# The attention's softmax: eight exponentials from PSUM with the negated maximum as bias, and carries by DMA

## The chip, the cores and the metric

One core of a Trainium2 chip runs the whole kernel in one launch. The metric is the device time in microseconds. TensorE multiplies matrices, VectorE and ScalarE work on tensors and read and write both SBUF and PSUM, GpSimd works on SBUF, and SyncE here only issues DMAs.

## The reference

The input x has four sequences of 1024 tokens with 128 features. It is layer-normalised to xn, and the output is x + A(xn) + F(xn). A is a retention block of 16 heads (a causal decaying product without softmax, with group norms and a small MLP). F is two layers of windowed attention with an MLP; each layer computes:

```python
h = shift_token(x)                       # half of the features from the token before
q, k, v = split(h @ wqkv)                # 8 heads of 64
q, k = rotary_xpos(l2norm(q) * qs, l2norm(k) * ks)
sim = q @ k.T * 8, masked to a window of 64 and the 64 before it
o = softmax(sim) @ v
x = x + o @ wo
h = layernorm(shift_token(x)) @ w1 + b1
x = x + (a * gelu(g)) @ w2 + b2          # a, g are the halves of h
```

## The kernel before, in words

All five engines run hand-written queues that meet at semaphores. Time is tiled in 8 steps of 128 tokens, and a step has four slots, one for each sequence (k = 0 to 3). `run_bodies` goes over 8 steps of layer 0, 8 of layer 1, and two bodies that drain. A body works on three steps at once: `new` (projections), `old` (attention output) and `ff` (the MLP). In slot k each engine does, among other things, the projection of tile k of the new step, the scores of the tile two slots back (`turned`) and the weighting with values of the tile three slots back (`weighted`).

On TensorE a slot is, in order: transposes of the normalised q and k (`pe_turn`, line 1040), the value projection (1135), mask and scores into the PSUM tile pS (`pe_scores`, 1059 and 1072), transposes of the softmax weights into pT (1083), transposes of the attention output (1109), the q and k projection into pQK (1172), the output projection (`pe_wo`, 1115), and weights times values, into pS again (`pe_values`, 1098). Slot 0 has the MLP's matmuls besides (1234, 1245). `pe_values` of one tile needs pS after the softmax of the next tile has read it, and the next slot's `pe_scores` needs pS after `dve_output` has read it.

On VectorE a slot is: the maximum over each head's 128 scores and its subtraction (`dve_scores`, 757 and 759, PSUM to the SBUF tile pr), the residual (779), the sum of squares of q and k (724), the division by the softmax sum (`dve_output`, 767 and 769), and two rotations of pQK (711). The sum of squares waits for ScalarE's `Square` of pQK (550).

On ScalarE a slot is: copies of kT and qT from pT (510, 512), two carries, the shifted input of the next slot (489), two copies of the values (526, 527), the copy prT of the turned weights (534), the copy oT of the turned output (590), the `Square` (550), and one `Exp` of 1024 columns in place in pr (583). In slot 0 the exponential stands before the table load and the gelus (597). In layer 0, slot 3 has four `Identity` instructions (570) at its start and the retention block's squares and copies (607, 612) around the `Square`, and the exponential of slot 3 stands inside the retention block (634), which follows the slot on all engines. In that block TensorE starts with transposes of `aqk` (1269), which VectorE makes (858) from GpSimd's power (385) of those squares. In slot 1 of layer 1 ScalarE has two `Silu` with a bias (646) and a table load besides.

The carries keep the last 64 tokens of a tile's keys and values for the next step's window: 64 partitions of `vown` to `vmix` (517), and 64 columns of `kT` (518). The copy of the values (526) waits for the first, the copy of kT (510) for the second. GpSimd computes the reciprocal norms by a power and scales q and k (353 to 375). SyncE loads the inputs at the start, then in layer 1 one input tile and one output tile a step.

Of the kernel before, what the change touches and what calls it, by code (L numbers as in the profile page):

```python
# [12 lines left out]
P = 128  # L13
NB = 4
# [79 lines left out]
def program(nc, a, out):  # L94
    with ExitStack() as ctx:
# [129 lines left out]
        def score_bank(b):  # L225
# [12 lines left out]
        gn = [{n: sem(f"gn{k}_{n}") for n in ("agg", "dve", "mm", "var", "rs", "done")} for k in range(2)]  # L238
        LS = {n: sem(n) for n in (
            "carried", "v_kept", "h_ready", "qk_mm", "v_mm", "sq_done", "ss_done", "mul_done", "max_ss", "rn_done", "add_done",  # L240
            "qkn_done", "t_mm", "t_ev", "v_ev", "s_mm", "mx_done", "sub_done", "exp_done",
            "pt_mm", "pt_ev", "o_mm", "rec_done", "o_done", "ot_mm", "ot_ev", "wo_mm", "xr_carried", "xr_done", "hs",
            "ln_mm", "ln_bst", "ln_st", "ln_eps", "ln_rs", "hn_done", "hnt_mm", "hnt_ev", "ag_mm", "gelu_done",
            "hf_done", "w2_mm", "x2_done")}
# [53 lines left out]
            body(None, None, (1, NT - 1))  # L298


        @block.sync
        def _(sp):
            for b in range(NB):
                sp.dma_start(x[:, b, :, :], a["L0_attn_x"][b].rearrange("(t p) d -> p t d", p=P)).then_inc(x_ld[b], 16)
            sp.dma_start(tab[:, :, :, :], a["k_tab"]).then_inc(tab_ld, 16)
            sp.dma_start(wqkv[:, 0, :], a["L0_ffn_wqkv"][0]).then_inc(wqkv_ld, 16)
            for l in range(DEPTH):
                sp.dma_start(w1[:, l, :], a["L0_ffn_w1"][l]).then_inc(w1_ld, 16)
            sp.dma_start(wqkv[:, 1, :], a["L0_ffn_wqkv"][1]).then_inc(w_ld, 16)
            for l in range(DEPTH):  # L310
                sp.dma_start(wo[:, l, :, :], a["L0_ffn_wo"][l].rearrange("(c p) d -> p c d", p=P)).then_inc(w_ld, 16)
                sp.dma_start(w2[:, l, 0:2, :], a["L0_ffn_w2"][l, 0:2 * P, :].rearrange("(c p) d -> p c d", p=P)).then_inc(w_ld, 16)
                sp.dma_start(w2[0:CHUNKS[2][1], l, 2, :], a["L0_ffn_w2"][l, 2 * P:HID, :]).then_inc(w_ld, 16)

            sp.dma_start(xs[:, :, :], x_steps[0]).then_inc(G["xs"], 16)
            sp.wait_ge(G["osb"], 1)
            sp.dma_start(out_steps[0], osb[:, :, :]).then_inc(G["out"], 16)
            with sp.Fori(1, NT) as t:
                sp.wait_ge(G["out"], 16 * t)
                sp.dma_start(xs[:, :, :], x_steps[t]).then_inc(G["xs"], 16)  # L320
                sp.wait_ge(G["osb"], t + 1)
                sp.dma_start(out_steps[t], osb[:, :, :]).then_inc(G["out"], 16)
            sp.wait_ge(G["out"], 16 * NT)


        def pool_slot(eng, new, old, k):

# [164 lines left out]
        def act_slot(eng, new, old, ff, k):  # L492
# [12 lines left out]
            if turned:  # L505
                step, b, m = turned
                eng.wait_ge(S["t_mm"], 2 * m + 1)
                if not is_start(step):
                    eng.wait_ge(S["carried"], m - 3)
                eng.activation(kT[b][:, :, 0:P], pT[:, 512:1024].rearrange("p (c n) -> p c n", c=4), ACT.Copy).then_inc(S["t_ev"], 1)  # L510
                eng.wait_ge(S["t_mm"], 2 * m + 2)
                eng.activation(qT[:, :, :], pT[:, 0:512].rearrange("p (c n) -> p c n", c=4), ACT.Copy).then_inc(S["t_ev"], 1)
            if new:
                if not is_start(new):

                    need(eng, S["o_mm"], n - 3)
                    eng.activation(vmix[k][64:P, :, 0:DH], vown[k][64:P, :, 0:DH], ACT.Copy).then_inc(S["v_kept"], 1)
                    eng.activation(kT[k][:, :, P:P + WIN], kT[k][:, :, WIN:P], ACT.Copy).then_inc(S["carried"], 1)
                if k < NB - 1:
                    act_shift(eng, new, k + 1)  # L520

                eng.wait_ge(S["v_mm"], n + 1)
                if not is_start(new):
                    eng.wait_ge(S["v_kept"], n - 3)
                values = pV[:, :].rearrange("p (h d) -> p h d", h=H)
                eng.activation(vown[k][:, :, 0:DH], values, ACT.Copy).then_inc(S["v_ev"], 1)
                eng.activation(vmix[k][0:64, :, 0:DH], values[0:64], ACT.Copy).then_inc(S["v_ev"], 1)
# [9 lines left out]
            if ff and k == 0:  # L537
                eng.wait_ge(S["hnt_mm"], step_count(ff) + 1)
                eng.activation(hnT[:, :], pM[:, :], ACT.Copy).then_inc(S["hnt_ev"], 1)
            if k == NB - 1 and new and new[0] == 0:  # L540
                act_retention_project(eng, new[1], 0)
            if k == 0 and turned:
                act_exp(eng, b, m)
            if k == 0 and ff:
                act_load_table(eng, ACT.Gelu)
                act_gelu(eng, ff, 0)
# [11 lines left out]
            if k == NB - 1 and new and new[0] == 0:  # L558
                act_retention_project(eng, new[1], 1)
            else:  # L560
                if old and k == NB - 1:
                    act_shift_residual(eng, old)
                if k > 0 and turned:
                    act_exp(eng, b, m)

        def act_retention_in(eng, t):

# [11 lines left out]
            eng.activation(hs[64:P, :, :], xr[64:P, :, 0:P], ACT.Copy).then_inc(S["hs"], 1)  # L579

        def act_exp(eng, b, n):
            eng.wait_ge(LS["sub_done"], n + 1)
            eng.activation(pr[:, b % 2, :, :], pr[:, b % 2, :, :], ACT.Exp).then_inc(LS["exp_done"], 1)  # L583

        def act_output(eng, step, b):

# [39 lines left out]
        def act_retention(eng, t, old):  # L626
            for k in range(NB):
                n = 4 * t + k
                eng.wait_ge(A["t_mm"], n + 1)
                need(eng, A["qx"], n - 1)  # L630
                eng.activation(aqkT[:, k % 2, :, :], pM[:, 0:256].rearrange("p (g n) -> p g n", g=2),
                               ACT.Copy).then_inc(A["t_ev"], 1)
                if k == 0:
                    act_exp(eng, 1, count((0, t), 1))
                act_place_values(eng, t, k)
                if k + 2 < NB:
                    act_retention_project(eng, t, k + 2)
                if k == 0 and old:
                    act_shift_residual(eng, old)
            eng.wait_ge(A["y_mm"], 4 * t + 4)  # L640
            eng.activation(ayT, pY, ACT.Copy).then_inc(A["yt"], 1)
# [110 lines left out]
        def dve_scores(eng, b, n):  # L752
# [1 line left out]
            S = LS  # L754
            eng.wait_ge(S["s_mm"], n + 1)
            sc = pS[:, :].rearrange("p (h n) -> p h n", h=H)
            eng.tensor_reduce(mx[:, :], sc, AX.X, ALU.max).then_inc(S["mx_done"], 1)  # L757
            eng.wait_ge(S["mx_done"], n + 1)
            eng.tensor_tensor(pr[:, b % 2, :, :], sc, mx[:, :].unsqueeze(2).broadcast_to([P, H, P]),  # L759
                              ALU.subtract).then_inc(S["sub_done"], 1)  # L760

        def dve_output(eng, n):

# [279 lines left out]
        def pe_scores(eng, step, b, n):  # L1043
# [2 lines left out]
            evicted, subtracted, weighed = (counted(eng, v) for v in (2 * n + 2, n, n - 1))  # L1046
            eng.wait_ge(mask_done, 1)
            eng.wait_ge(S["t_ev"], evicted)
            need(eng, S["sub_done"], subtracted)
            need(eng, S["o_done"], weighed)  # L1050
            if b == 2:

# [33 lines left out]
        def pe_values(eng, b, n, turned):  # L1086
# [2 lines left out]
            eng.wait_ge(S["pt_ev"], n + 1)  # L1089
            eng.wait_ge(S["v_ev"], 2 * n + 2)  # L1090
            if turned:
                eng.wait_ge(S["sub_done"], n + 2)
            need(eng, S["o_done"], n)
            for i in range(H):
                g, j = i // 4, i % 4
# [125 lines left out]
        def pe_hidden(eng, step, chunks, turned, weighted):  # L1221
            S, l, ct = LS, step[0], step_count(step)
            for k in chunks:
# [3 lines left out]
                    if weighted:  # L1227
                        eng.wait_ge(S["pt_ev"], weighted[2] + 1)
                if k == 1 and turned:
                    eng.wait_ge(S["sub_done"], turned[2] + 1)  # L1230
                if k == 2:
                    eng.wait_ge(S["hf_done"], NC * ct + 1)
                for s in range(2):
# [190 lines left out]
```

## Time and profile before

| what | value |
|---|---|
| median of 3 runs | 990.7 us (988.4 to 990.86) |
| the profiled execution, its time | 988.95 us |
| its span, first to last instruction | 986.8 us |
| mean granted TensorE clock | 0.980 |
| TensorE busy | 868.8 us, 88% |
| VectorE busy | 685.1 us, 69% |
| ScalarE busy | 691.4 us, 70% |
| GpSimd busy | 623.8 us, 63% |

The profile is one execution. Its page has the busy time of each engine and groups of instructions by line; the trace behind it can be asked for who waited for whom, for windows, and for a timeline. A wait is put to the instruction that ended it. Durations of neighbouring instructions on one engine overlap, so the time that one really takes of its engine is from its start to the start of the next.

### The profile page before, as it was taken

How to read it: one execution, taken by the hardware profiler on the slowest of the kernel's cores; microseconds unless marked ns; L12 is line 12 of the kernel's file. 1: busy time of each engine (PE TensorE's matmuls, PEld its weight loads, DVE VectorE, ACT ScalarE, POOL GpSimd, SP SyncE). 2: the span in 40 equal slices, each digit the busy share in tenths (PEclk: the TensorE clock that was granted, in tenths of full speed). 3: DMA queues.
4: the chain of work that ended last, by engine and by line, in shares of the span. 5: the costliest groups of instructions: out<-in, count | busy, mean ns of one | idle time of the engine just before them, and what ended most of it. 6: DMA issues, size and time to landing. Idle time of an engine off the chain costs nothing.

```text
span 986.8 us, 26415 instructions
## 1 busy us (share of the span) xinstructions
PE 868.8 (88%) x10836; PEld 582.5 (59%) x10836; DVE 685.1 (69%) x1129; ACT 691.4 (70%) x1419; POOL 623.8 (63%) x492
## 2 busy tenths in 40 slices
PE   1678889989899998998989889999999999999876
PEld 0346666666656666566666656565656565656552
DVE  5874665757667576675666877888787878797733
ACT  0456786877868777687786667777777777777643
POOL 4488676776767767767576566657575757575500
PEclk9979999999999999999999899999999999999987
DMA  9100000000000000000000000000000000000000
GB/s 291 28 1 3 2 2 2 2 3 2 3 2 1 3 1 3 2 2 3 1 3 2 1 1 2 2 12 12 13 12 7 17 2 22 1 23 2 22 23 11
DMA packets 20481, 13.47 MB, mean 14 GB/s; under 512 B 4578, under 2 KB 19596, under 8 KB 20236
## 3 DMA queue, kind: packets, MB, share of 16 engines
q1 hardware_dynamic: 15108, 10.49, 3.5%
q10 hardware_dynamic: 5256, 1.31, 0.8%
q8 instruction: 87, 1.43, 0.6%
q14 instruction: 30, 0.25, 0.1%
HBM read 9.70 MB, written 2.10 MB: 12 GB/s over the span
## 4 chain that ended last, share of the span: by engine, by line
PE 51%; DVE 23%; ACT 14%; issue 8%; POOL 3%; DMA 1%; DVEq 0%; POOLq 0%; SPq 0%; ACTq 0%
PE pQK L1172 6%; DVE m L711 6%; PE pS L1098 5%; PE pT L1083 4%; PE pT L1040 4%; PE pM L1115 4%; PE pV L1135 4%; PE pM L1245 4%; PE pS L1072 4%; PE pQK L1336 3%; DVE xa L899 2%; DVE ss L724 2%; DVE pr L759 2%; DVE mx L757 2%; PE pS L1059 2%
## 5 line engine op out<-in xcount | busy, mean ns | idle before, releaser
L355 POOL TENSOR_TENSOR rn<-rn,half_neg 128x16 f32<-128x16 f32 x64 | 187.5, 2929 | 5.3
L368 POOL TENSOR_TENSOR m<-m 128x1024 f32<-128x1024 f32 x64 | 151.0, 2359 | 1.0 <-DVE m L711 1.0
L353 POOL TENSOR_SCALAR rn<-ss 128x16 f32<-128x16 f32 x64 | 16.3, 255 | 205.1 <-DVE ss L724 203.9
L375 POOL TENSOR_TENSOR qkn<-m,rn 128x1024 f32<-128x1024 f32 x64 | 123.7, 1933 | 5.0
L757 DVE TENSOR_REDUCE mx<-pS 128x8 f32<-128x1024 f32 x64 | 78.1, 1220 | 66.7 <-PE pS L1072 66.6
L1172 PE MATMUL pQK<-wqkv,hT 128*128 128x512 f32 x256 | 123.5, 606 | 0.8 <-DVE m L711 0.8
L510 ACT ACTIVATE kT<-pT 128x512 f32<-128x512 f32 x64 | 38.1, 595 | 86.4 <-PE pT L1040 85.9
L550 ACT ACTIVATE sq<-pQK 128x1024 f32<-128x1024 f32 x64 | 65.4, 1021 | 25.7 <-PE pQK L1172 25.6
L724 DVE TENSOR_REDUCE ss<-sq 128x16 f32<-128x1024 f32 x64 | 77.5, 1210 | 5.4 <-ACT sq L550 5.3
L1098 PE MATMUL pS<-vmix,prT 128*64 128x65 f32 x1024 | 74.0, 226 | 7.4 <-DVE pr L759 7.4
L1098 PEld LDWEIGHTS pS<-vmix,prT 128*64 128x64 f32 x1024 | 65.3, 139 | 25.5 <-issue 20.8
L759 DVE TENSOR_TENSOR pr<-pS,mx 128x1024 f32<-128x1024 f32 x64 | 78.4, 1225 | 2.2
L534 ACT ACTIVATE prT<-pT 128x1024 f32<-128x1024 f32 x64 | 65.1, 1017 | 18.4 <-PE pT L1083 17.9
L583 ACT ACTIVATE pr<-pr 128x1024 f32<-128x1024 f32 x64 | 67.7, 1058 | 13.6 <-DVE pr L759 12.6
L711 DVE TENSOR_TENSOR m<-pQK,rope 128x1024 f32<-128x1024 f32 x64 | 76.2, 1215 | 0.0
L1135 PE MATMUL pV<-wqkv,hT 128*128 128x512 f32 x128 | 69.8, 628 | 6.9 <-DVE gst L940 2.9
L711 DVE TENSOR_TENSOR m<-pQK,tab 128x1024 f32<-128x1024 f32 x64 | 75.4, 1210 | 0.0
L1098 PE MATMUL pS<-vown,prT 128*64 128x65 f32 x1024 | 74.2, 226 | 0.0
L1040 PE MATMUL pT<-cst,qkn 128*128 128x128 f32 x512 | 69.7, 280 | 4.6 <-POOL qkn L375 4.6
L1083 PE MATMUL pT<-cst,pr 128*128 128x128 f32 x512 | 69.9, 279 | 0.0
L1072 PE MATMUL pS<-kT,qT 64*64 64x128 f32 x2048 | 68.5, 272 | 0.0
L1234 PE MATMUL pT<-hnT,w 128*128 128x512 f32 (+1 forms) x128 | 63.9, 624 | 4.9 <-DVE hidden L841 3.5
(169 smaller groups left out, 2038.2 us busy)
## 6 DMA issues: line engine op xcount, KB each, us to landing
x<-in_L_attn_x SPq DMA_DIRECT2D x4, 512.0 KB, 9.4
xs<-in_L_attn_x SPq DMA_DIRECT2D x8, 256.0 KB, 2.8
out<-aqkT SPq DMA_DIRECT2D x8, 256.0 KB, 2.2
wqkv<-in_L_ffn_wqkv SPq DMA_DIRECT2D x2, 768.0 KB, 9.5
tab<-in_k_tab SPq DMA_DIRECT2D x1, 1024.0 KB, 10.5
w<-in_L_ffn_w SPq DMA_DIRECT2D x2, 341.0 KB, 10.3
wo<-in_L_ffn_wo SPq DMA_DIRECT2D x2, 256.0 KB
cst<-in_k_cst ACTq DMA_DIRECT2D x1, 404.5 KB, 4.0
```

The costliest lines, as they stand in the source:

```text
L355: eng.tensor_tensor(rn[:, k % 2, :], rn[:, k % 2, :], half_neg[:, 0:2 * H], ALU.pow).then_inc(S["rn_done"], 1)
L368: eng.tensor_tensor(m1[:, k % 2, :], m1[:, k % 2, :], m2[:, :], ALU.add).then_inc(S["add_done"], 1)
L375: eng.tensor_tensor(qkn[:, k % 2, :].rearrange("p (h d) -> p h d", d=DH), m1[:, k % 2, :].rearrange("p (h d) -> p h d", d=DH), rn[:, k % 2 ...
L711: eng.tensor_tensor(m.rearrange(shape, g=2, h=H, **sizes), src, by, ALU.mult).then_inc(S["mul_done"], 1)
L757: eng.tensor_reduce(mx[:, :], sc, AX.X, ALU.max).then_inc(S["mx_done"], 1)
L759: eng.tensor_tensor(pr[:, b % 2, :, :], sc, mx[:, :].unsqueeze(2).broadcast_to([P, H, P]), ALU.subtract).then_inc(S["sub_done"], 1)
L1040: mm = eng.transpose(pT[:, j * P:(j + 1) * P], qkn[:, b % 2, j * P:(j + 1) * P], ident)
L1072: mm = eng.matmul(pS[64 * w:64 * w + 64, col0:col0 + P], qT[r, j, 64 * w:64 * w + 64], keys, start=False, stop=True, skip_group_check=True)
L1083: mm = eng.transpose(pT[:, j * P:(j + 1) * P], pr[:, b % 2, j, :], ident)
L1098: mm = eng.matmul(pS[64 * w:64 * w + 64, col0:col0 + DH + 1], prT[:, i, 64 * w:64 * w + 64], (vown if w else vmix)[b][:, 2 * j + g, :], st ...
L1135: eng.matmul(pV[:, :], hT[:, k, :], wqkv[:, l, 1024:1536], start=True, stop=True).then_inc(S["v_mm"], 1)
L1172: mm = eng.matmul(pQK[:, g * 512:(g + 1) * 512], hT[:, k, :], wqkv[:, l, g * 512:(g + 1) * 512], start=True, stop=True)
```

## The change

Four edits, made together.

1. `dve_scores` keeps only the maximum, now negated. It first waits until the exponentials of the tile before are done, since they read mx.
2. `act_exp` waits for the maximum and issues eight `Exp` instructions of 128 columns, one a head, from pS to pr, with that head's column of mx as bias. Whatever waited for the subtraction (`pe_scores`, `pe_values`, `pe_hidden`) now waits for the eighth of these.
3. In `act_slot` the exponentials stand right after oT, ahead of the retention projections and the `Square`, in every slot; the one inside the retention block moves to slot 3.
4. The two carries of a slot leave ScalarE and become DMAs from SBUF to SBUF on SyncE's queue, the first behind the `pe_values`, the second behind the scores of the same sequence a step before. SyncE's loop over input and output tiles is written out by bodies for that.

```diff
+        def sp_carry(sp, n, b):
+            sp.wait_ge(LS["o_mm"], n - 3)
+            sp.dma_start(vmix[b][64:P, :, :], vown[b][64:P, :, :]).then_inc(LS["v_kept"], 16)
+            sp.wait_ge(LS["s_mm"], n - 3)
+            sp.dma_start(kT[b][:, :, P:P + WIN], kT[b][:, :, WIN:P]).then_inc(LS["carried"], 16)
...
-            with sp.Fori(1, NT) as t:
-                sp.wait_ge(G["out"], 16 * t)
-                sp.dma_start(xs[:, :, :], x_steps[t]).then_inc(G["xs"], 16)
-                sp.wait_ge(G["osb"], t + 1)
-                sp.dma_start(out_steps[t], osb[:, :, :]).then_inc(G["out"], 16)
+            def body(new, old, ff):
+                last = ff and ff[0] == 1
+                if last:
+                    need(sp, G["out"], 16 * ff[1])
+                    sp.dma_start(xs[:, :, :], x_steps[ff[1]]).then_inc(G["xs"], 16)
+                for k in range(NB):
+                    if new and not is_start(new):
+                        sp_carry(sp, count(new, k), k)
+                if last:
+                    sp.wait_ge(G["osb"], ff[1] + 1)
+                    sp.dma_start(out_steps[ff[1]], osb[:, :, :]).then_inc(G["out"], 16)
...
-                    need(eng, S["o_mm"], n - 3)
-                    eng.activation(vmix[k][64:P, :, 0:DH], vown[k][64:P, :, 0:DH], ACT.Copy).then_inc(S["v_kept"], 1)
-                    eng.activation(kT[k][:, :, P:P + WIN], kT[k][:, :, WIN:P], ACT.Copy).then_inc(S["carried"], 1)
...
+            if turned:
+                act_exp(eng, b, m)
             if k == NB - 1 and new and new[0] == 0:
                 act_retention_project(eng, new[1], 0)
-            if k == 0 and turned:
-                act_exp(eng, b, m)
...
-                if k > 0 and turned:
-                    act_exp(eng, b, m)
...
         def act_exp(eng, b, n):
-            eng.wait_ge(LS["sub_done"], n + 1)
-            eng.activation(pr[:, b % 2, :, :], pr[:, b % 2, :, :], ACT.Exp).then_inc(LS["exp_done"], 1)
+            eng.wait_ge(LS["mx_done"], n + 1)
+            for h in range(H):
+                weights = eng.activation(pr[:, b % 2, h, :], pS[:, h * P:(h + 1) * P], ACT.Exp, bias=mx[:, h:h + 1])
+            weights.then_inc(LS["exp_done"], 1)
...
-                if k == 0:
-                    act_exp(eng, 1, count((0, t), 1))
...
-            eng.tensor_reduce(mx[:, :], sc, AX.X, ALU.max).then_inc(S["mx_done"], 1)
-            eng.wait_ge(S["mx_done"], n + 1)
-            eng.tensor_tensor(pr[:, b % 2, :, :], sc, mx[:, :].unsqueeze(2).broadcast_to([P, H, P]),
-                              ALU.subtract).then_inc(S["sub_done"], 1)
+            need(eng, S["exp_done"], n)
+            eng.tensor_reduce(mx[:, :], sc, AX.X, ALU.max, negate=True).then_inc(S["mx_done"], 1)
...
             if turned:
-                eng.wait_ge(S["sub_done"], n + 2)
+                eng.wait_ge(S["exp_done"], n + 2)
```

## Rows read from the trace of the kernel before

**Rows 1.** The page: busy time, share of the span, instructions.

```profile
PE 868.8 (88%) x10836; PEld 582.5 (59%) x10836; DVE 685.1 (69%) x1129; ACT 691.4 (70%) x1419; POOL 623.8 (63%) x492
```

**Rows 2.** The waits: who waited for whom, us, times, longest.

```profile
PE pS L1098 <- DVE pr L759: 7.4, 8, 3.8
```

**Rows 3.** Windows of a step of each layer: busy by engine, PEclk, DMA.

```profile
401.30:462.80 61.50, 57.74 (x908) 40.21 (x903) 40.51 (x70) 47.93 (x116) 43.46 (x38) 1.00 0.01 2
...
701.00:751.00 50.00, 47.05 (x448) 30.33 (x447) 40.31 (x56) 37.79 (x62) 31.43 (x20) 1.00 0.04 12
```

**Rows 4.** Groups by line and shape: busy us, mean ns, idle before.

```profile
L759 DVE TENSOR_TENSOR pr<-pS,mx 128x1024 f32<-128x1024 f32 x64 | 78.4, 1225 | 2.2
...
L583 ACT ACTIVATE pr<-pr 128x1024 f32<-128x1024 f32 x64 | 67.7, 1058 | 13.6 <-DVE pr L759 12.6
...
L526 ACT ACTIVATE vown<-pV 128x512 f32<-128x512 f32 x64 | 38.0, 594 | 7.7 <-PE pV L1135 6.7
...
L570 ACT ACTIVATE xa<-xnT,gsh,gsc 128x128 f32<-128x128 f32 x32 | 13.1, 480 | 0.0
...
L646 ACT ACTIVATE avm<-pQK,col 128x512 f32<-128x512 f32 x16 | 10.3, 685 | 2.0 <-PE pQK L1141 1.9
...
L607 ACT ACTIVATE asq<-pV 128x128 f32<-128x128 f32 x32 | 8.9, 279 | 0.7
```

**Rows 5.** Timeline of ScalarE, start of slot 3, layer 0: start, us.

```profile
432.65 1.64 ACT L570 ACTIVATE xa<-xnT,gsh,gsc 128x128 f32<-128x128 f32 x4
```

**Rows 6.** Timeline of ScalarE, layer 0, slots 1 and 3.

```profile
421.30 0.59 ACT L590 ACTIVATE oT<-pM 128x512 f32<-128x512 f32 x1
...
439.09 0.28 ACT L607 ACTIVATE asq<-pV 128x128 f32<-128x128 f32 x1
```

**Rows 7.** Timeline of VectorE: layer 0 from 423, layer 1 from 698.

```profile
423.48 1.21 DVE L724 TENSOR_REDUCE ss<-sq 128x16 f32<-128x1024 f32 x1
...
427.71 1.22 DVE L757 TENSOR_REDUCE mx<-pS 128x8 f32<-128x1024 f32 x1
...
698.37 1.21 DVE L724 TENSOR_REDUCE ss<-sq 128x16 f32<-128x1024 f32 x1
...
705.74 1.21 DVE L757 TENSOR_REDUCE mx<-pS 128x8 f32<-128x1024 f32 x1
...
708.39 1.21 DVE L724 TENSOR_REDUCE ss<-sq 128x16 f32<-128x1024 f32 x1
...
713.37 1.22 DVE L757 TENSOR_REDUCE mx<-pS 128x8 f32<-128x1024 f32 x1
...
717.48 1.21 DVE L724 TENSOR_REDUCE ss<-sq 128x16 f32<-128x1024 f32 x1
...
724.36 1.22 DVE L757 TENSOR_REDUCE mx<-pS 128x8 f32<-128x1024 f32 x1
```

**Rows 8.** Timeline of TensorE: first `pe_values` matmul of slots, and two more.

```profile
423.17 0.27 PE L1098 MATMUL pS<-vmix,prT 128*64 128x65 f32 x1
...
431.42 0.27 PE L1098 MATMUL pS<-vmix,prT 128*64 128x65 f32 x1
...
443.00 0.44 PE L1269 MATMUL pM<-cst,aqk 128*128 128x128 f32 x2
...
698.06 0.27 PE L1098 MATMUL pS<-vmix,prT 128*64 128x65 f32 x1
...
708.47 0.24 PE L1098 MATMUL pS<-vmix,prT 128*64 128x65 f32 x1 [0.33 <-DVE pr L759]
...
717.16 0.27 PE L1098 MATMUL pS<-vmix,prT 128*64 128x65 f32 x1
...
746.94 1.16 PE L1115 MATMUL pM<-oT,wo 128*128 128x128 f32 x8 [0.69 <-ACT oT L590]
...
748.03 0.27 PE L1098 MATMUL pS<-vmix,prT 128*64 128x65 f32 x1
```

**Rows 9.** The page: DMA issues, KB each, us to landing.

```profile
out<-aqkT SPq DMA_DIRECT2D x8, 256.0 KB, 2.2
```

More of the change, by code:

```diff
@@ L240, in program @@
             "carried", "v_kept", "h_ready", "qk_mm", "v_mm", "sq_done", "ss_done", "mul_done", "max_ss", "rn_done", "add_done",
-            "qkn_done", "t_mm", "t_ev", "v_ev", "s_mm", "mx_done", "sub_done", "exp_done",
+            "qkn_done", "t_mm", "t_ev", "v_ev", "s_mm", "mx_done", "exp_done",
             "pt_mm", "pt_ev", "o_mm", "rec_done", "o_done", "ot_mm", "ot_ev", "wo_mm", "xr_carried", "xr_done", "hs",
@@ L313, in _ @@
                 sp.dma_start(w2[0:CHUNKS[2][1], l, 2, :], a["L0_ffn_w2"][l, 2 * P:HID, :]).then_inc(w_ld, 16)
-            sp.dma_start(xs[:, :, :], x_steps[0]).then_inc(G["xs"], 16)
-            sp.wait_ge(G["osb"], 1)
-            sp.dma_start(out_steps[0], osb[:, :, :]).then_inc(G["out"], 16)
-            with sp.Fori(1, NT) as t:
-                sp.wait_ge(G["out"], 16 * t)
-                sp.dma_start(xs[:, :, :], x_steps[t]).then_inc(G["xs"], 16)
-                sp.wait_ge(G["osb"], t + 1)
-                sp.dma_start(out_steps[t], osb[:, :, :]).then_inc(G["out"], 16)
+            def body(new, old, ff):
[9 more added lines that the diff above has]
+                    sp.dma_start(out_steps[ff[1]], osb[:, :, :]).then_inc(G["out"], 16)
+            run_bodies(sp, body)
             sp.wait_ge(G["out"], 16 * NT)
@@ L508, in act_slot @@
                 if not is_start(step):
-                    eng.wait_ge(S["carried"], m - 3)
+                    eng.wait_ge(S["carried"], 16 * (m - 3))
                 eng.activation(kT[b][:, :, 0:P], pT[:, 512:1024].rearrange("p (c n) -> p c n", c=4), ACT.Copy).then_inc(S["t_ev"], 1)
@@ L513, in act_slot @@
             if new:
-                if not is_start(new):
-                    need(eng, S["o_mm"], n - 3)
-                    eng.activation(vmix[k][64:P, :, 0:DH], vown[k][64:P, :, 0:DH], ACT.Copy).then_inc(S["v_kept"], 1)
-                    eng.activation(kT[k][:, :, P:P + WIN], kT[k][:, :, WIN:P], ACT.Copy).then_inc(S["carried"], 1)
                 if k < NB - 1:
@@ L523, in act_slot @@
                 if not is_start(new):
-                    eng.wait_ge(S["v_kept"], n - 3)
+                    eng.wait_ge(S["v_kept"], 16 * (n - 3))
                 values = pV[:, :].rearrange("p (h d) -> p h d", h=H)
@@ L1048, in pe_scores @@
             eng.wait_ge(S["t_ev"], evicted)
-            need(eng, S["sub_done"], subtracted)
+            need(eng, S["exp_done"], subtracted)
             need(eng, S["o_done"], weighed)
@@ L1229, in pe_hidden @@
                 if k == 1 and turned:
-                    eng.wait_ge(S["sub_done"], turned[2] + 1)
+                    eng.wait_ge(S["exp_done"], turned[2] + 1)
                 if k == 2:
```

## The prediction

> **What bounds the kernel now.** I read the page first. TensorE is busy for 868.8 of 986.8 us, the other engines for 63 to 70% [rows 1]. So a gain must shorten a wait of TensorE, and work taken off VectorE or ScalarE is worth only what TensorE waited for it. Second, the list of waits: VectorE's subtraction (line 759) holds the matmuls of `pe_values` (line 1098) for 7.4 us in all, and in slot 1 of layer 1 TensorE waits 0.69 us for ScalarE's `oT` copy [rows 2, 8]. The first figure is all that TensorE now pays for the step that is rewritten. Third, the windows of one step of each layer: TensorE is busy 57.74 of 61.5 us in layer 0 and 47.05 of 50 us in layer 1 [rows 3]. It has next to no slack, so whatever arrives later than now moves the end. Last, the timelines of single slots, from which the sum comes. A slot handles one batch element of each stage of the pipeline, four slots make a step, and in layer 0 the retention block follows slot 3.
>
> **What the edit costs by the piece.** VectorE loses one subtraction per tile, 64 times 1.225 us = 78.4 us; the maximum stays, and I take its negation as free: the subtraction reads the same 1024 columns, adds arithmetic and a write of 1024 to them, and is timed by the columns alone, at 1.2 ns each [rows 4]. Dearer than one more such pass, 1.2 us, it can't well be; cheaper than now neither. ScalarE loses the two carry copies of each slot and one exponential of 1.058 us, and gets eight of 128 columns from PSUM with a pointer as bias. No row has that form. The `Square` of 128 columns from PSUM without a pointer takes 279 ns. A pointer adds 91 ns: 685 ns for the `Silu` of 512 columns with a bias at line 646 against 594 for the copy of 512 from PSUM. The `Identity` with two pointers takes 480 ns for 128 columns, which leaves about 388 for one. Four of these stand in 1.64 us, so they start every (1.64 - 0.48) / 3 = 0.387 us and overlap by 0.093 [rows 4, 5]. One exponential is then 0.38 us, the next starts after 0.285, and eight take 7 x 0.285 + 0.38 = 2.38 us: 1.3 us more than the one. Bounds: no less than the one exponential over all 1024 columns, 1.06 us [rows 4], and at the 0.387 us of two pointers 7 x 0.387 + 0.48 = 3.2 us [rows 5]. I take 2.38, since both one-pointer estimates meet there. The Trainium skill (ScalarE: Activation LUTs, section "What ACT_TABLE_LOAD costs") speaks against the change the same way: each pointer operand adds about 93 ns to a fixed part that every ACTIVATE pays again, and neighbours overlap by 93 ns. By it eight exponentials would be 2.44 us, an estimate from that page, and the total below some 4 us higher; the 91 ns between 685 and 594 agree.
>
> **Where this lies on the path.** Three edits matter together. PSUM's score tile is now free for `pe_values` only after the exponentials (`exp_done` for `sub_done`, line 1092). The exponentials stand ahead of the `Square` of the query and key tile (line 550) on ScalarE. And VectorE's sum of squares (line 724) waits for that `Square` and stands ahead of the output scaling, the rotations and the next maximum. That makes a ring through two engines: end of the exponentials, `Square`, sum of squares, output, two rotations, maximum, next exponentials. From the end of one group to the next it takes 0.96 us until the sum starts (a `Square` starts a tenth before the last exponential ends, and lasts 1.02), then what stands on VectorE from the sum to the next maximum, then 1.25 us for the maximum, then 2.38.
>
> Layer 0, slot 1. The `oT` copy starts at 421.30; it lasts a good 0.4 us until the next may start, so the exponentials run from 421.7 to 424.1, where `pe_values` now starts at 423.17: 0.9 us late [rows 6, 8]. To slot 2: VectorE needs 427.71 - 423.48 = 4.23 us from sum to maximum [rows 7], so the ring takes 0.96 + 4.23 + 1.25 + 2.38 = 8.82 us, against 431.42 - 423.17 = 8.25 for TensorE's own work [rows 8]: 0.6 more, 1.5 together. In slot 3 ScalarE's four `Identity` rows come first, `Square` being late, and they delay the scores by 1.1. The maximum is then at 432.9 + 0.96 + 4.23 = 438.1 and done at 439.4; the scores end at 437.7, the transposes behind them at 438.7, `prT` and `oT` follow in 1.4 us, and the exponentials hold ScalarE from 440.15 to 442.5. `pe_values` is 1.1 late, but behind it on ScalarE stand the two retention squares, now at 439.09 and then at 442.5, 3.4 us late [rows 6]. Their consumers follow in line: GpSimd's power, VectorE's `aqk`, the transposes on TensorE, now at 443.00 [rows 8]; these had some 0.8 us in hand, and the first rotation and the residual, which slip behind, don't stand in their way: 445.0 to 445.6, and I take 445.0. The exponential that stood inside the retention block (line 634) is gone and gives 0.95 us back to ScalarE. Followed through its four rounds, TensorE is 2.0 to 2.8 us late and leaves the block 2.25 late. In slot 0 the gelu path waits: the exponentials end 2.38 - 1.06 = 1.3 us later, then come table load, gelu and `hidden`, and TensorE, which has some 0.3 us in hand there, loses 1.05 in its waits for `hidden`. A step of layer 0 grows by 3.3 us.
>
> Layer 1. From slot 1 to 2 VectorE has `dve_block_out` between: 705.74 - 698.37 = 7.37 us [rows 7], so the ring takes 0.96 + 7.37 + 1.25 + 2.38 = 11.96 us against 708.47 - 698.06 = 10.41: +1.55. From 2 to 3: 713.37 - 708.39 = 4.98, ring 9.57 against 717.16 - 708.47 = 8.69: +0.9 [rows 7, 8]. From 3 over 0 back to 1: to the end of slot 0's exponentials 0.96 + 6.88 + 1.25 + 2.38 = 11.5; table load, gelu and `hidden` 2.9; then TensorE's own work until the block's w1 matmuls, and ScalarE's `Silu`, table load, `prT` and `oT` 14.0; the exponentials 2.4. Together 30.8, against 748.03 - 717.16 = 30.9: nothing lost, because taking the carries out of slot 1 removes the wait of 0.69 us for `oT` and the cover that is left absorbs the rest. A step grows by 2.4 us.
>
> **The carries on SyncE's queue.** Each slot gets two transfers between SBUF regions. The critical one is `vmix`, issued after the previous step's `pe_values` and needed by ScalarE's `vown` copy. In layer 0, slot 2, the `pe_values` before ends at 424.1 + 1.1 = 425.2 in the new timing. The scores wait for the output scaling until 427.1, take 1.25 us and the transposed weights another 1.0, so `prT` can't start before 429.35, and the two `vown` and `vmix` copies ahead of it (0.5 us each) may start at 428.3: 3.1 us of cover. If that cover is gone, `prT`, `oT` and the exponentials are late by the same amount. The nearest row lands in 2.2 us, for twice the bytes [rows 9], so I cost it at nothing; if a landing takes 4.0 us, nearly twice that row, each is 0.9 us late. The key carry waits for scores two slots old and has a slot and more. The queue's other users in layer 1 are one load and one store a step; the store of a step now stands behind slot 3's carries, which are ready before its own input, and its landing must be seen before slot 0's carry, whose condition comes some 4 us later.
>
> **The sum.** Layer 0: 7 steps x 3.3 = 23.1, and 2 for the first, which has two scored slots and the block. Layer 1: 8 x 2.4 = 19.2, and 2 for the last two bodies and the change of layers, where the maximum waits for the group statistics and the eight exponentials follow it bare. Total 46.3 us on the profiled execution's 988.95 us gives 1035.3. That execution is 1.75 us below the median of 990.7, so I say 1036 us. What a measurement of this kernel can tell from no change is about 0.3%, 3 us.
>
> **The rivals.**
> Cheap exponentials (0.07 for faster, 0.05 for no change). If short instructions hide their start so well that eight take as long as one, the mechanism above vanishes: the ring of layer 0 is 7.5 us, under 8.25, and the wait for `oT`, 0.69 us in slot 1 by the list, and `pe_values`' 0.33 in slot 2 go in six steps. That gives 6 us, so 983. It decides at 1.8 us for eight, where layer 0's ring meets TensorE's 8.25; at 1.4 us layer 1 still pays 0.55 us in slot 2 and the time is about 988. For it: ScalarE's rows do overlap, by a tenth of a microsecond. against it: the pointer's 91 ns in two independent rows, and four `Identity` rows that take 1.64 us for half the columns.
> Late carries (0.08). With landings of 4 us some 45 slots wait 0.9 us each: 40 us on top, 1075. For it: the key carry's pieces are 256 bytes long where the store's are 512. Against it: half the bytes, a queue that has nothing else to do, and the critical carry's rows of 2,080 bytes.
> Absorbed later: the delays of slots 2 and 3 are eaten by waits in the block. The sums above hold this already for the 0.89 us stall before slot 3's scores; full absorption of layer 0 would give 1012. It is inside my case's range.
>
> The forecast case has 0.80, and its own range is 1012 to 1060: the per-instruction cost at 0.265 to 0.31 us moves it by 10 us either way, the hand-followed block by as much again. Faster 0.07, same 0.05, slower 0.88. The range 1010 to 1060 leaves out the rivals on both sides.
>
> **What would show it.** Eight `pr<-pS` rows of about 0.38 us, 2.4 us together; VectorE near 607 us busy and ScalarE near 691 - 68 + 152 = 775 less the carries; `pe_values` waiting for `pr` of ScalarE in slots 1 to 3; the sum of squares no longer under the wait for `pM` but for `sq`; GpSimd's wait unchanged in kind; steps of 64.8 and 52.4 us. I am wrong if the exponentials start less than 0.22 us apart, if TensorE's waits name the carries, or if the step of layer 0 stays at 61.5.

## The result, and the profile after

The changed kernel takes 1040.55 us (median of 4 runs, 1039.13 to 1043.05) against 990.19 us before: a ratio of 1.0514, with a 95% interval from 1.0489 to 1.054. The forecast was 1036 us, 4.5 us under it, and the range of 1010 to 1060 holds it.

The page of the changed kernel, first lines, answers to [rows 1]:

```profile
span 1039.2 us, 26806 instructions
...
PE 873.5 (84%) x10836; PEld 584.4 (56%) x10836; DVE 615.9 (59%) x1065; ACT 700.4 (67%) x1747; POOL 623.7 (60%) x492
```

VectorE gave up 69 us of busy time, not the 78 forecast, because busy time counts the overlap of neighbours once: a subtraction had 1.08 us to itself. TensorE gave up none: its work is the same, its busy time 4.7 us longer, and the span around it is 52.4 us longer. The groups by line, with their busy time, mean, and the idle time before them:

```profile
L588 ACT ACTIVATE pr<-pS,mx 128x128 f32<-128x128 f32 x512 | 139.0, 388 | 13.3 <-DVE mx L762 12.5
...
L762 DVE TENSOR_REDUCE mx<-pS 128x8 f32<-128x1024 f32 x64 | 78.0, 1219 | 64.8 <-PE pS L1074 64.7
...
L728 DVE TENSOR_REDUCE ss<-sq 128x16 f32<-128x1024 f32 x64 | 78.0, 1219 | 65.8 <-ACT sq L556 65.7
...
L1100 PE MATMUL pS<-vmix,prT 128*64 128x65 f32 x1024 | 73.8, 226 | 46.9 <-ACT pr L588 46.9
```

One exponential lasts 388 ns, so 512 last 199 us, but they overlap and occupy ScalarE for 139 us, 2.17 us a tile. The last row is most of the loss: in [rows 2] the matmuls of `pe_values` waited 7.4 us for the subtraction, now they wait 46.9 us for the exponentials. The negated maximum costs 1219 ns, as the plain one did. The windows of a step, as in [rows 3]:

```profile
425.30:489.90 64.60, 58.01 (x901) 40.05 (x900) 35.73 (x65) 48.28 (x136) 42.73 (x36) 1.00 0.08 19
707.10:759.40 52.30, 46.76 (x448) 30.38 (x448) 36.59 (x51) 38.18 (x83) 31.36 (x19) 1.00 0.13 32
```

A step of layer 0 went from 61.5 to 64.6 us, one of layer 1 from 50 to 52.3. The timeline of TensorE, first `pe_values` matmul of slots 1 and 2 of layer 0, then of slots 3, 1, 2 and 3 of layer 1, is what [rows 8] showed before:

```profile
445.27 0.24 PE L1100 MATMUL pS<-vmix,prT 128*64 128x65 f32 x1 [0.95 <-ACT pr L588]
...
454.55 0.24 PE L1100 MATMUL pS<-vmix,prT 128*64 128x65 f32 x1 [0.95 <-ACT pr L588]
...
707.11 0.24 PE L1100 MATMUL pS<-vmix,prT 128*64 128x65 f32 x1 [0.64 <-ACT pr L588]
...
738.07 0.24 PE L1100 MATMUL pS<-vmix,prT 128*64 128x65 f32 x1 [0.95 <-ACT pr L588]
...
749.80 0.24 PE L1100 MATMUL pS<-vmix,prT 128*64 128x65 f32 x1 [1.65 <-ACT pr L588]
...
759.38 0.24 PE L1100 MATMUL pS<-vmix,prT 128*64 128x65 f32 x1 [0.64 <-ACT pr L588]
```

The bracket at the end of a row is the wait and who ended it. In layer 1 the distances are 31.0, 11.7 and 9.6 us; the prediction's were 30.8, 12.0 and 9.6. In layer 0 the distance from slot 1 to slot 2 is 9.28 us where it said 8.82. The chain of work between these two slots shows by what the 9.28 is made:

```profile
445.27 1.15 PE pS L1100 x32
446.42 1.02 PE pT L1042 x8
447.45 0.86 PE pV L1137 x2
448.31 0.34 PE pS L1061 x4
448.65 0.87 PE pS L1074 x32
449.52 1.04 PE pT L1085 x8
...
450.58 1.02 ACT prT L540
451.61 0.49 ACT oT L596
...
452.12 0.04 ACT pr L588
...
452.89 1.41 ACT pr L588 x5
```

VectorE is not in it. The ring closes through TensorE: `pe_values`, the next slot's transposes and value projection, scores, transposes of the weights, then prT and oT on ScalarE, and behind them the eight exponentials, which the next `pe_values` waits for. The same chain, through prT, makes the 9.6 us from slot 2 to 3 of layer 1. In layer 1 from slot 1 to 2, where VectorE has `dve_block_out` to do, it does pass through VectorE, as forecast. The timeline of ScalarE there shows the exponentials waiting for the maximum:

```profile
746.07 0.59 ACT L596 ACTIVATE oT<-pM 128x512 f32<-128x512 f32 x1
747.38 2.17 ACT L588 ACTIVATE pr<-pS,mx 128x128 f32<-128x128 f32 x8 [0.72 <-DVE mx L762]
749.39 1.07 ACT L556 ACTIVATE sq<-pQK 128x1024 f32<-128x1024 f32 x1
```

The carries, in the page's list of DMA issues, beside [rows 9]:

```profile
vmix<-vown SPq DMA_DIRECT2D x60, 130.0 KB, 2.2
kT<-kT SPq DMA_DIRECT2D x60, 128.0 KB, 2.3
```

They land in 2.2 and 2.3 us, and ScalarE's `vown` copy waits 3.6 us for them in the whole kernel.

### The profile page after: what moved, and what is told of

It is laid out like the page before. It is cut to its first block, busy times and chain, and to the rows that moved or that the text cites. A ratio compares the mean times of both kernels' runs of the same rounds, so it can differ in the third digit from the quotient of the medians.

```text
span 1039.2 us, 26806 instructions
## 1 busy us (share of the span) xinstructions
PE 873.5 (84%) x10836; PEld 584.4 (56%) x10836; DVE 615.9 (59%) x1065; ACT 700.4 (67%) x1747; POOL 623.7 (60%) x492
## 4 chain that ended last, share of the span: by engine, by line
PE 35%; ACT 27%; DVE 23%; issue 10%; POOL 3%; DMA 1%; DVEq 0%; POOLq 0%; SPq 0%; ACTq 0%
ACT pr L588 11%; DVE m L715 7%; PE pT L1085 4%; ACT prT L540 4%; PE pS L1074 4%; PE pS L1100 4%; PE pT L1042 4%; PE pM L1247 3%; PE pV L1137 3%; DVE xa L901 3%; ACT sq L556 3%; PE pQK L1338 3%; DVE ss L728 2%; ACT oT L596 2%; DVE mx L762 2%
## 5 line engine op out<-in xcount | busy, mean ns | idle before, releaser
L588 ACT ACTIVATE pr<-pS,mx 128x128 f32<-128x128 f32 x512 | 139.0, 388 | 13.3 <-DVE mx L762 12.5
L728 DVE TENSOR_REDUCE ss<-sq 128x16 f32<-128x1024 f32 x64 | 78.0, 1219 | 65.8 <-ACT sq L556 65.7
L762 DVE TENSOR_REDUCE mx<-pS 128x8 f32<-128x1024 f32 x64 | 78.0, 1219 | 64.8 <-PE pS L1074 64.7
L1100 PE MATMUL pS<-vmix,prT 128*64 128x65 f32 x1024 | 73.8, 226 | 46.9 <-ACT pr L588 46.9
L556 ACT ACTIVATE sq<-pQK 128x1024 f32<-128x1024 f32 x64 | 67.5, 1054 | 6.5 <-PE pQK L1174 6.5
L1174 PEld LDWEIGHTS pQK<-wqkv,hT 128*128 128x128 f32 x256 | 45.4, 195 | 38.3 <-issue 32.7
```

Of the source, the lines that this page charges most:

```text
L588: weights = eng.activation(pr[:, b % 2, h, :], pS[:, h * P:(h + 1) * P], ACT.Exp, bias=mx[:, h:h + 1])
L1100: mm = eng.matmul(pS[64 * w:64 * w + 64, col0:col0 + DH + 1], prT[:, i, 64 * w:64 * w + 64], (vown if w else vmix)[b][:, 2 * j + g, :], st ...
L1174: mm = eng.matmul(pQK[:, g * 512:(g + 1) * 512], hT[:, k, :], wqkv[:, l, g * 512:(g + 1) * 512], start=True, stop=True)
```

## The experiments

The kernel before took 989.6 to 990.0 us beside each set of runs. All ratios below are to it.

### Each half of the change alone

The kernel before with the carries by DMA, and nothing else:

```diff
-                    eng.activation(vmix[k][64:P, :, 0:DH], vown[k][64:P, :, 0:DH], ACT.Copy).then_inc(S["v_kept"], 1)
-                    eng.activation(kT[k][:, :, P:P + WIN], kT[k][:, :, WIN:P], ACT.Copy).then_inc(S["carried"], 1)
...
+            sp.dma_start(vmix[b][64:P, :, :], vown[b][64:P, :, :]).then_inc(LS["v_kept"], 16)
...
+            sp.dma_start(kT[b][:, :, P:P + WIN], kT[b][:, :, WIN:P]).then_inc(LS["carried"], 16)
```

> The kernel before with edit 4 alone: the carries by DMA on SyncE's queue, softmax as before. Theory (the eight exponentials are the loss): the carries cost nothing and take the 0.69 us wait for oT out of slot 1 of layer 1, so 984 to 991 us. Rival (the carries land late or disturb other queues): 1000 us or more, with ScalarE's vown copy waiting for the DMA for tens of us.

Measured: 984.14 us, ratio 0.9938 (0.9914 to 0.9961). The carries are a gain of 5.5 us; the time is at the lower end of the expected band. In slot 1 of layer 1 TensorE no longer waits for oT.

The changed kernel with the carries back on ScalarE:

```diff
-            sp.dma_start(vmix[b][64:P, :, :], vown[b][64:P, :, :]).then_inc(LS["v_kept"], 16)
...
-            sp.dma_start(kT[b][:, :, P:P + WIN], kT[b][:, :, WIN:P]).then_inc(LS["carried"], 16)
...
+                    eng.activation(vmix[k][64:P, :, 0:DH], vown[k][64:P, :, 0:DH], ACT.Copy).then_inc(S["v_kept"], 1)
+                    eng.activation(kT[k][:, :, P:P + WIN], kT[k][:, :, WIN:P], ACT.Copy).then_inc(S["carried"], 1)
```

> The changed kernel with the carries back on ScalarE: edits 1 to 3 without 4. Theory: all of the loss stays, and a little comes on top where ScalarE's 1.0 us of carries a slot does not fit into its wait for the turned weights: 1041 to 1052 us. Rival (the DMA carries make the loss): back to 990 to 1000 us.

Measured: 1053.6 us, ratio 1.0636 (1.0606 to 1.0665), a little above the expected band. The softmax edit alone costs 64 us, and the carries by DMA give 13 of them back, more than twice what they give to the kernel before. That ScalarE now has less slack for them is the likely reason, and was not taken apart. Rival "late carries" falls.

### The place of the exponentials on ScalarE

The eight exponentials behind the `Square` again, but for slot 0 and slot 3 of layer 0:

```diff
-            if turned:
+            retain = k == NB - 1 and new and new[0] == 0
+            if turned and (k == 0 or retain):
                 act_exp(eng, b, m)
...
                     act_shift_residual(eng, old)
+                if k > 0 and turned:
+                    act_exp(eng, b, m)
```

> The changed kernel with the eight exponentials behind the Square again in slots 1 and 2 of both layers and slot 3 of layer 1, as before; slot 3 of layer 0 and slot 0 as in the change. Theory (pe_values waits for the exponentials, through ScalarE's order): they then end 1 to 1.5 us later still behind pQK and the Square, and pe_values with them, so 1065 to 1090 us. Rival (the late Square and VectorE's late sum of squares make the loss, not pe_values): the sum starts on time again and the time falls below 1030 us.

Measured: 1142.72 us, ratio 1.1541 (1.1514 to 1.1568). The sign is that of the theory and the size is far beyond it. `pe_values` waits 115.0 us for the exponentials, 68 more than in the changed kernel, and the time is 102 us longer. Part of what the waits leave open is probably TensorE's clock, which granted 0.90 in the mean from 600 to 900 us (0.99 in the changed kernel). The first matmul behind a gap of this kernel, by TensorE's timeline:

```profile
470.29 0.34 PE L1103 MATMUL pS<-vmix,prT 128*64 128x65 f32 x1 [2.62 <-ACT pr L591]
...
470.43 0.32 PE L1103 MATMUL pS<-vmix,prT 128*64 128x65 f32 x1
```

They take 0.32 us where they took 0.22 in the kernel before, and the granted clock from 470 to 480 us is 0.84: behind a stand (idle stretch) of 2.6 us they run at a lower clock. So the place that the change chose, ahead of the `Square`, is by far the better one for these eight instructions. The sum of squares waits only 9.5 us for the `Square` here, for 65.7 in the changed kernel, and the time is longer all the same: a late sum isn't what costs.

### How many instructions

One maximum over all heads of a token and a single Exp, whose edit is shown; then one for each pair of heads and four; then sixteen, two a head with that head's own maximum:

```diff
-            for h in range(H):
-                weights = eng.activation(pr[:, b % 2, h, :], pS[:, h * P:(h + 1) * P], ACT.Exp, bias=mx[:, h:h + 1])
+            for h in range(1):
+                weights = eng.activation(pr[:, b % 2, 8 * h:8 * h + 8, :], pS[:, h * 8 * P:(h + 1) * 8 * P].rearrange("p (h n) -> p h n", h=8), ACT.Exp,
+                                         bias=mx[:, h:h + 1])
...
-            sc = pS[:, :].rearrange("p (h n) -> p h n", h=H)
+            sc = pS[:, :].rearrange("p (h n) -> p h n", h=1)
...
-            eng.tensor_reduce(mx[:, :], sc, AX.X, ALU.max, negate=True).then_inc(S["mx_done"], 1)
+            eng.tensor_reduce(mx[:, 0:1], sc, AX.X, ALU.max, negate=True).then_inc(S["mx_done"], 1)
```

> The changed kernel with one maximum for all eight heads of a token and one Exp of 1024 columns from PSUM with that one pointer as bias. A shift common to all heads cancels in the softmax as each head's own does; what is left out is only each head's own protection from underflow. Theory (it is the eight fixed parts): the exponential takes 1.15 us for 2.17, the ring falls to TensorE's own 8.2 us in layer 0, and the time to 978 to 991 us. Rival (the order on ScalarE or the carries, not the number of instructions): 1020 us or more.

> The changed kernel with one maximum for each pair of heads and four Exp of 256 columns. A shift common to two heads cancels in the softmax. The eight Exp rows of the changed kernel start 0.255 us apart and last 0.39; with 128 more columns at 0.83 ns that is 3 x 0.36 + 0.49 = 1.58 us for the four, against 2.17 for eight and 1.12 for one. Theory (each fixed part counts, until TensorE's own work hides the rest): 995 to 1012 us; by a straight line between one and eight it would be 1009. Rival (only the number being one matters): above 1020 us.

> The changed kernel with sixteen Exp of 64 columns, two a head with the same pointer: the same elements, twice the number of instructions. One, four and eight gave 984.6, 1007.1 and 1040.6 us at 1.12, 1.58 and 2.17 us for the exponentials. Theory (64 times, each further microsecond of exponentials costs about 57 us in all once TensorE waits for them): 64 columns less take 0.053 us off a start, so 15 x 0.20 + 0.33 = 3.3 us for the sixteen, and 1090 to 1120 us, more if TensorE's clock falls in the longer gaps. Rival (the loss of the eight is the order on ScalarE and would not grow): 1040 to 1050 us.

| exponentials a tile | on ScalarE, us a tile | time, us | ratio (interval) |
|---|---|---|---|
| 1 of 1024 columns | 1.12 | 984.64 | 0.9951 (0.9938 to 0.9964) |
| 4 of 256 | 1.57 | 1007.14 | 1.0191 (1.0172 to 1.021) |
| 8 of 128 (the change) | 2.17 | 1040.55 | 1.0514 (1.0489 to 1.054) |
| 16 of 64 | 3.39 | 1137.68 | 1.1491 (1.1461 to 1.1521) |

The single Exp is back at the time of the DMA carries alone, 984.14 us: with one instruction the softmax edit costs nothing, and gains nothing either. From one to eight each microsecond on ScalarE costs 55.91 / 1.05 = 53 us, for 64 tiles: most of what is added arrives. From eight to sixteen it is 97.13 / 1.22 = 80 us, and the time is above the expected band; the mean granted clock of this kernel is 0.948, against 0.977, and how much of the excess is the clock was not taken apart.

These kernels also show the ring of layer 0, slot 1 to slot 2. By the chain above it is 6.85 us from `pe_values` to the first exponential (445.27 to 452.12), then the group, then 0.26 us to the next `pe_values`. For four exponentials of 1.57 us together that gives 8.68, and TensorE's timeline of that kernel has 8.67:

```profile
429.17 0.24 PE L1101 MATMUL pS<-vmix,prT 128*64 128x65 f32 x1 [0.35 <-ACT pr L588]
...
437.84 0.24 PE L1101 MATMUL pS<-vmix,prT 128*64 128x65 f32 x1 [0.35 <-ACT pr L588]
```

The prediction's ring through VectorE would give 0.96 + 4.23 + 1.25 + 1.57 = 8.01 us, and TensorE's own 8.25 would have hidden it. For the single Exp the chain gives 8.23, and the distance is back at 8.25 (423.83, 432.08), with no wait. The groups of the two extremes by line:

```profile
L588 ACT ACTIVATE pr<-pS,mx 128x1024 f32<-128x1024 f32 x64 | 71.4, 1116 | 13.1 <-DVE mx L763 12.3
```

```profile
L588 ACT ACTIVATE pr<-pS,mx 128x64 f32<-128x64 f32 x1024 | 217.1, 369 | 12.3 <-DVE mx L763 11.5
```

Half the columns (64 for 128) make an instruction 19 ns shorter, 369 for 388. Most of it is fixed.

### The pointer

The eight Exp without a bias; the maximum is computed and waited for, and no shift is applied:

```diff
-                weights = eng.activation(pr[:, b % 2, h, :], pS[:, h * P:(h + 1) * P], ACT.Exp, bias=mx[:, h:h + 1])
+                weights = eng.activation(pr[:, b % 2, h, :], pS[:, h * P:(h + 1) * P], ACT.Exp)
```

> The changed kernel with the eight Exp without a pointer: the maximum is still computed and waited for, but nothing is subtracted, so each head's shift is left out. It parts the pointer's price from that of the number of instructions. Theory (a pointer costs 0.09 us of each start, the rest is the fixed part): the starts 0.16 us apart, eight in 1.4 to 1.5 us, and 990 to 1004 us. Rival (the 0.255 us between starts are the instruction's own, whatever its bias): 1035 to 1045 us.

Measured: 999.0 us, ratio 1.0088 (1.0073 to 1.0103). The timeline of ScalarE has the eight in one row:

```profile
443.21 1.47 ACT L588 ACTIVATE pr<-pS 128x128 f32<-128x128 f32 x8
```

Without the pointer eight take 1.47 us for 2.17, so a pointer costs 0.70 / 8 = 0.09 us of each, as the two rows of before had said. It is 41.6 of the 55.9 us between eight and one. The other 14.4 part eight without a pointer from one that still has its pointer; one with a maximum and without a pointer was not run.

### The maximum, and with one Exp the place

The eight Exp with a pointer to a constant and no maximum; then one Exp, no pointer and no maximum; then that with the carries on ScalarE (edit shown above). The second and third leave out the shift that guards the exponential against overflow; a constant one stands for it in the first.

```diff
-            eng.wait_ge(LS["mx_done"], n + 1)
+            eng.wait_ge(LS["s_mm"], n + 1)
...
-                weights = eng.activation(pr[:, b % 2, h, :], pS[:, h * P:(h + 1) * P], ACT.Exp, bias=mx[:, h:h + 1])
+                weights = eng.activation(pr[:, b % 2, h, :], pS[:, h * P:(h + 1) * P], ACT.Exp, bias=half_neg[:, 0:1])
...
-            if turned:
-                dve_scores(eng, turned[1], turned[2])
```

The second and third have the first's new wait and no `dve_scores` either, and one Exp:

```diff
-            for h in range(H):
-                weights = eng.activation(pr[:, b % 2, h, :], pS[:, h * P:(h + 1) * P], ACT.Exp, bias=mx[:, h:h + 1])
-            weights.then_inc(LS["exp_done"], 1)
+            eng.activation(pr[:, b % 2, :, :], pS[:, :].rearrange("p (h n) -> p h n", h=H), ACT.Exp).then_inc(LS["exp_done"], 1)
```

> The changed kernel with its eight Exp, with a pointer to a column that holds one constant for all heads (it cancels), and no maximum: ScalarE waits for the scores alone. It parts the maximum on VectorE from the eight instructions. Theory (prT and oT on ScalarE are the last to be done before the exponentials in most slots, and the maximum only where the list says so, 12.5 us in all): 1022 to 1034 us. Rival (VectorE's ring, as the prediction drew it, with the maximum's 1.2 us on it in three slots of four): under 1000 us.

> The changed kernel without any maximum: VectorE does nothing between the scores and the exponential, and ScalarE takes one Exp of 1024 columns from PSUM as soon as the scores are there. The shift against overflow is left out. Theory (with one exponential the maximum is hidden behind prT and oT on ScalarE in most slots, and TensorE's own work is the bound): 972 to 984 us, a little under the kernel with one maximum. Rival (VectorE's load still sets the pace in slots 1 and 2 of layer 1): below 965 us.

> The kernel without a maximum and with one Exp, with the carries back on ScalarE. It prices the carries where the exponentials no longer hold TensorE. They cost 13 us in the changed kernel and 5.5 us in the kernel before. Theory (they cost where ScalarE is late for oT and the scores): 968 to 976 us. Rival (carries are free once the exponentials are short): 963 to 967 us.

Measured: 1025.82 us for the first, ratio 1.0368 (1.0344 to 1.0392): 14.7 us under the changed kernel, inside the expected band and close to the 12.5 us that the list of waits names for the maximum. The other 35.8 us over the kernel before stay, with no maximum in the kernel at all. The first `pe_values` matmuls of slots 1 and 2 of layer 0, then of slots 1, 2 and 3 of layer 1, by this kernel's timeline of TensorE:

```profile
444.12 0.24 PE L1098 MATMUL pS<-vmix,prT 128*64 128x65 f32 x1 [0.95 <-ACT pr L588]
...
453.40 0.24 PE L1098 MATMUL pS<-vmix,prT 128*64 128x65 f32 x1 [0.95 <-ACT pr L588]
...
726.94 0.24 PE L1098 MATMUL pS<-vmix,prT 128*64 128x65 f32 x1 [0.95 <-ACT pr L588]
...
737.98 0.24 PE L1098 MATMUL pS<-vmix,prT 128*64 128x65 f32 x1 [0.95 <-ACT pr L588]
...
747.55 0.24 PE L1098 MATMUL pS<-vmix,prT 128*64 128x65 f32 x1 [0.65 <-ACT pr L588]
```

The distances are 9.28, 11.04 and 9.57 us, for 9.28, 11.73 and 9.58 in the changed kernel. Without the 1.2 us of a maximum on VectorE only the middle one, slot 1 to 2 of layer 1, gets shorter, by 0.69. So VectorE's ring binds there and in neither of the other two slots in which the prediction drew it.

Measured for the second: 965.21 us, ratio 0.9755 (0.9742 to 0.9769), the fastest kernel of the study, under its expected band and 0.2 us above its rival's bound. 19.4 us go against the single Exp with a maximum. The edit also takes the pointer off and 1.2 us a tile off VectorE, and these were not parted; from slot 1 to 2 of layer 1 the distance falls from 10.65 us (698.59, 709.24) to 10.01 (686.13, 696.14), so there the rival's mechanism, VectorE's load, did still count. Measured for the third: 973.78 us, ratio 0.9839 (0.9816 to 0.9862), as expected: the carries by DMA are worth 8.6 us there.

One Exp with its pointer, behind the `Square` as in the place experiment above:

> The kernel with one maximum and one Exp, and that Exp behind the Square again in slots 1 and 2 and in slot 3 of layer 1. Theory (pe_values now waits for the exponential itself, so its place decides): 1.1 us behind the Square, 1.3 us late in each of these slots, 1010 to 1035 us. Rival (the place matters only where eight instructions stand there): 980 to 990 us.

Measured: 1047.09 us, ratio 1.0584 (1.057 to 1.0599), above the expected band and over the 984.64 us of the single Exp ahead of the `Square`: 62 us for the place alone. Its `pe_values` waits 73.9 us for the exponential. The kernel before could afford this place, since pS was free for `pe_values` with the subtraction, and the exponential in SBUF held no use of pS.

## Why the prediction was right

**The cost of the eight.** It took 0.38 us each, 0.285 apart, 2.38 together. Measured: 0.388 each and 2.17 together, so (2.17 - 0.388) / 7 = 0.255 apart. The duration was right; they overlap by 0.13 us, not by the 0.093 of the four `Identity` rows. By the page of the Trainium skill cited there (ScalarE: Activation LUTs, "What ACT_TABLE_LOAD costs") one takes 387 ns, an estimate from its formula for 128 columns and a pointer, and the trace agrees with 388; it gives an overlap of 93 ns, and there the trace doesn't agree.

**The path.** That `pe_values` would wait for the exponentials is shown by the 46.9 us in the list and by the counts: one instruction takes the whole softmax loss away, sixteen more than double it. That was the mechanism, and it was right. The ring that prices it was not: it was drawn through VectorE, and only in layer 1 from slot 1 to slot 2 does it run there. In layer 0 it runs through TensorE and ScalarE's prT and oT, and two errors met: the exponentials are 0.21 us cheaper, and they start 0.67 us later behind the maximum than the 1.25 assumed (452.12 - 450.20 = 1.92), for oT is the last to be done. That gives 9.28 for 8.82 us, the 0.46 that the slot is off. In slot 3 the exponentials start 6.99 us behind slot 2's `pe_values` (461.54) for the 7.23 of the prediction, and the retention squares 2.00 behind them for 2.35, so the squares are 18.3 us behind slot 1's `pe_values` for 18.4, and the step of layer 0 came out at 64.6 for 64.8. That the 0.46 is gone by then is luck: cheaper exponentials and a longer way to them cancel.

**Layer 1.** A step of 52.3 us for 52.4, and here too a part is luck. From slot 2 to 3 the 9.57 us that were drawn through VectorE are matched to 0.01 us by the other ring, as the kernel without a maximum shows. That slots 3 over 0 to 1 lose nothing is seen in the 31.0 us between 707.11 and 738.07, against 30.9 before. The prediction led that stretch through slot 0's exponentials, table load and gelu; the gelu is done at 720.2 us, but by the chain it is VectorE, busy with the group norm's scale (line 901) until 720.3, that starts `hidden` at 720.43. The two ways end within 0.2 us of each other.

**The sum.** It had 46.3 us, and 50.4 were measured, 52.4 by the spans. How far the `pe_values` of the changed kernel stand behind those of the kernel before, by the two timelines of TensorE, says which terms were off:

| slot 1 of | before | after | behind | added, and forecast |
|---|---|---|---|---|
| the second step of layer 0 | 113.66 | 119.48 | 5.8 | 5.8 for 2 |
| the first step of layer 1 | 546.17 | 574.76 | 28.6 | 22.8 for 7 x 3.3 = 23.1 |
| the third step of layer 1 | 648.09 | 685.80 | 37.7 | 9.1 for 2 x 2.4, and a share of 2 |
| the last step of layer 1 | 897.96 | 947.17 | 49.2 | 11.5 for 5 x 2.4 = 12 |
| the first of the last two bodies | 945.56 | 997.97 | 52.4 | 3.2 for 2.4, and a share of 2 |

The seven steps of layer 0 are right in sum, and a regular step of layer 1 adds 2.3 us for 2.4. The term that was too small is "2 for the first step and 2 for the change of layers and the last bodies": by the table the first is 5.8 and the second 4.3 + 0.8 = 5.1. At the start it isn't the length of the eight that costs: the kernel's very first `pe_values` comes at 78.47 for 74.86, and with a single Exp at 78.23. With the DMA carries alone, where the softmax is as before, it is at 77.05, so a part of it has nothing to do with the exponentials; what it is stays open. Two more rows show the same. The first step's output projection of the retention block (TensorE's timeline) moved from 94.86 to 99.02, 4.2 us for 2. And the second step of layer 1 cost 7.7 us: VectorE's `hn` rows of its slot 0 and the next stand 46.98 us apart before (576.16, 623.14) and 54.68 after:

```profile
606.27 1.36 DVE L836 TENSOR_SCALAR hn<-pM,lmv,lrs 128x128 f32<-128x128 f32 x4
...
660.95 1.36 DVE L836 TENSOR_SCALAR hn<-pM,lmv,lrs 128x128 f32<-128x128 f32 x4
```

There the group norm's shift (line 953) stands before the maximum, ScalarE waits 1.99 us for the maximum, and TensorE waits 2.92 us for `pe_values` (1.68 in the kernel before, at 608.97), by its timeline and windows:

```profile
644.13 0.30 PE L1100 MATMUL pS<-vmix,prT 128*64 128x65 f32 x1 [2.92 <-ACT pr L588]
```

```profile
640.00:645.00 5.00, 2.08 (x26) 1.76 (x26) 2.01 (x4) 3.08 (x9) 2.28 (x2) 0.92 0.01 2
645.00:650.00 5.00, 5.00 (x68) 3.88 (x65) 4.20 (x5) 2.27 (x4) 3.74 (x3) 0.74 0.43 108
```

The granted clock falls to 0.74 behind the gap, which makes the stall dearer than its length. How much of the 7.7 us is the clock and how much the wait was not taken apart. That both come through the maximum is shown by the kernel without one: from slot 1 of the first step of layer 1 to that of the third it takes 101.1 us (574.22, 675.36), for 111.0 in the changed kernel and 101.9 in the one before. The prediction named this place ("the maximum waits for the group statistics") and gave it a share of 2 us; it is 9.1, and some 10 of the 14.7 us that the kernel without a maximum gains.

**The carries.** Costed at nothing inside the loss, and taking oT's wait away: right in kind, for they land in 2.2 us. But they are a gain of their own, 5.5 us in the kernel before and 13 beside the new softmax. The prediction had the carries inside its sum and never stated a gain for them.

**The rivals.** "Cheap exponentials" named the point from which the sign turns as 1.8 us for eight, and 983 us below it. The break-even lies lower: at 1.57 us the kernel is still 1.9% slower, at 1.47 still 0.9%, at 1.12 0.5% faster. The ring through prT and oT is the reason in layer 0: with 6.85 + 0.26 us around the group it meets TensorE's 8.25 at 1.14 us, not at 1.8, and the kernels of one and four exponentials bear it out. "Late carries" didn't occur. "Absorbed later" didn't either: a step of layer 0 grew by 3.1 us for the 3.3 forecast.

## What to carry to other kernels

Before an operation is moved from one wide instruction to several narrow ones on another engine, multiply the fixed part and ask who waits for the last of them: here an exponential in SBUF that held nobody became one in PSUM that held the bank for TensorE. When a ring of waits is drawn, draw it through every engine that stands in order before the moved instruction, its own engine's earlier work too (prT and oT), and take the longest. A change made of two parts should be timed in parts: the carries alone are a gain of 0.6%, and the softmax was only worth having as a single instruction without a pointer and a maximum.

## What the runs showed of the hardware

A stand of TensorE of 2.6 to 5.0 us was followed by a lower granted clock: `pe_values` matmuls of 0.32 us instead of 0.22 behind 2.62 us at 470.29 us of the kernel with the late exponentials; 0.74 from 645 to 650 us behind 2.92 us in the changed one; and there too 0.70 from 590 to 595 us behind 4.99 us. Behind waits of 0.6 to 1.65 us in the changed kernel's steps the clock stayed at 1.00 in the windows shown, and behind 1.68 us in the kernel before it was 1.00 from 610 to 615 us. The kernels with sixteen exponentials and with the late eight have mean granted clocks of 0.948 and 0.934, which is part of their time; how large a part was not measured.

Narrow instructions didn't get shorter with their columns: 388 ns for an Exp of 128 columns with a pointer, 369 for 64, where the columns alone would take off 53 at the 0.83 ns each that the copies of 512 and 1024 show.

In slots 1 and 2 of layer 0 the first exponential doesn't start before oT has ended: oT starts at 451.50 and lasts 0.59 us, the Exp starts at 452.12, though the maximum was done at 451.42. In slot 3 of layer 1 it starts 0.48 us behind the start of oT (756.47, 756.95) and overlaps it. In slot 3 of layer 0 (461.07, 461.54) and, without pointers, in slot 2 of layer 0 (433.87, 434.34) it overlaps too. What parts the cases wasn't tested.
